# V of a pair of tiles as two-by-two blocks with seven products in place of eight

## The reference

```
q, k, v = heads(x @ Wq + bq), heads(x @ Wk + bk), heads(x @ Wv + bv)
scores  = einsum('bhqd,bhkd->bhqk', q, k) * scale
attn    = softmax(where(adj == 0, -inf, scores))
out     = einsum('bhqk,bhkd->bhqd', attn, v) as rows @ Wo + bo
result  = layernorm(x + out)          # eps 1e-5, no weight, no bias
```

## Time and profile before

| what | value |
|---|---|
| runs, median (lowest to highest) of 3 | 821.98 us (821.61 to 822.32) |
| the profiled execution | 821.39 us |
| its span, first to last instruction | 819.5 us |
| TensorE busy | 812.0 us, 99% |
| VectorE busy | 544.9 us, 66% |
| GpSimd busy | 512.6 us, 63% |
| ScalarE busy | 238.2 us, 29% |

### The profile page before, as it was taken

How to read it: one execution, slowest core, us unless ns; L and a number is a source line. 1 busy time by engine, 2 the same in 40 slices (tenths; PEclk the granted TensorE clock), 3 DMA queues, 4 the chain that set the end, 5 groups by cost and what they waited for, 6 DMA issues and landing times.

```text
span 819.5 us, 25422 instructions
## 1 busy us (share of the span) xinstructions
PE 812.0 (99%) x11286; PEld 665.1 (81%) x11286; DVE 544.9 (66%) x691; ACT 238.2 (29%) x315; POOL 512.6 (63%) x407
## 2 busy tenths in 40 slices
PE   9999999999999999999999999999999999999997
PEld 7788888888888888888888888888888888888886
DVE  5667667766567666676665776656766567766795
ACT  6532233221332222332223322133322233223223
POOL 1386667656675565856658566576665767657682
PEclk9999999999999999999999999999999999999999
DMA  9224424253342433424334243352424434234342
GB/s 321 90 79 122 120 81 135 84 143 95 88 143 72 149 92 92 139 70 142 105 91 134 71 144 95 82 154 82 128 88 106 136 82 131 84 108 118 105 105 104
DMA packets 50173, 92.37 MB, mean 113 GB/s; under 512 B 11280, under 2 KB 13328, under 8 KB 47888
## 3 DMA queue, kind: packets, MB, share of 16 engines
q1 hardware_dynamic: 47568, 87.08, 36.2%
q10 hardware_dynamic: 2496, 3.67, 1.6%
HBM read 40.37 MB, written 16.78 MB: 70 GB/s over the span
## 4 chain that ended last, share of the span: by engine, by line
PE 98%; DVE 1%; POOL 0%; ACT 0%; issue 0%; POOLq 0%; DVEq 0%
PE ring L289 23%; PE ring L291 21%; PE ring L290 21%; PE ring L386 7%; PE ring L387 7%; PE ring L390 7%; PE psum_s L357 6%; PE ring L375 6%; PE ring L407 1%; PE ring L309 0%; POOL soft L912 0%; PE ring L313 0%; PE ring L317 0%; DVE soft L717 0%; DVE top L724 0%; ACT soft L568 0%
## 5 line engine op out<-in xcount | busy, mean ns | idle before, releaser
L912 POOL TENSOR_TENSOR soft<-soft,top 128x1024 f32<-128x1024 f32 x62 | 125.2, 2020 | 77.5 <-DVE top L724 77.5
L171 POOL TENSOR_TENSOR soft<-soft,inverse 128x1024 f32<-128x1024 f32 x62 | 118.9, 1918 | 24.9 <-DVE inverse L731 22.2
L563 ACT ACTIVATE kt<-ring,bk 128x512 f32<-128x512 f32 x64 | 43.6, 681 | 258.7 <-PE ring L291 258.6
L889 POOL TENSOR_TENSOR x_lo<-x_raw,x_hi 128x512 fp32r<-128x512 f32 x56 | 72.0, 1286 | 61.1 <-ACT x_hi L548 61.1
L289 PE MATMUL ring<-wv_hi,x_hi 128*128 128x512 f32 x256 | 103.5, 404 | 0.0
L289 PE MATMUL ring<-x_hi,wk_hi 128*128 128x512 f32 x256 | 103.1, 403 | 0.0
L728 DVE TENSOR_REDUCE total<-soft 128x16 f32<-128x1024 f32 x62 | 75.6, 1219 | 41.0 <-ACT soft L568 41.0
L291 PE MATMUL ring<-wv_hi,x_lo 128*128 128x512 f32 x256 | 100.1, 391 | 0.0
L291 PE MATMUL ring<-x_hi,wk_lo 128*128 128x512 f32 x256 | 99.9, 390 | 0.0
L290 PE MATMUL ring<-x_lo,wk_hi 128*128 128x512 f32 x256 | 99.7, 390 | 0.0
L290 PE MATMUL ring<-wv_lo,x_hi 128*128 128x512 f32 x256 | 99.6, 389 | 0.0
(11 more groups left out here) (81 smaller groups left out, 1362.3 us busy)
## 6 DMA issues: line engine op xcount, KB each, us to landing
pt<-soft SPq DMA_DIRECT2D x464, 64.0 KB, 2.0
x_raw<-in_xt SPq DMA_DIRECT2D x15, 1024.0 KB, 6.8
row<-in_x SPq DMA_DIRECT2D x60, 256.0 KB, 2.7
out_rows<-row SPq DMA_DIRECT2D x60, 256.0 KB, 2.6
adj<-in_adj SPq DMA_DIRECT2D x16, 128.0 KB, 2.9
pt<-soft ACTq DMA_DIRECT2D x32, 64.0 KB, 2.2
kt<-in_wk SPq DMA_DIRECT2D x4, 256.0 KB, 5.1
row<-in_wv SPq DMA_DIRECT2D x1, 1024.0 KB, 8.4
```

The source lines that it names most:

```text
L171: ops.tensor_tensor(soft_of(c), soft_of(c), on_keys(inverse[:, c % 2, :]), ALU.mult).then_inc(normed, 1)
L889: nc.gpsimd.tensor_tensor(x_lo[:, buf, :, rows], x_raw[:, :, rows], x_hi[:, buf, :, rows].bitcast(F32), ALU.subtract).then_inc(x_lo_done, 1)
L912: nc.gpsimd.tensor_tensor(soft_of(c), soft_of(c), on_keys(top[:, c % 2, :]), ALU.subtract).then_inc(centred, 1)
```

## The change

For the pairs 1 to 27 (SEVEN), V of a pair is a product of two-by-two blocks: the rows of the two tiles by the two halves of the 512 input features, times the two halves of those by the two halves of the 512 output columns (HALF = 256). Seven block products, each of sums and differences of blocks, take the place of eight. One block product is six matmuls of 256 columns.

The sums of weights (t_raw, from Wv) are made once at the start by GpSimd (add_weights), in pt's space, cast by ScalarE and subtracted by VectorE. The sums of inputs are made for each pair: SP loads the pair's columns of the transposed x a second time (load_pair, 512 KB) into the two buffers of v that the pair will use (s_raw), VectorE makes four sums in place (add_inputs), ScalarE casts them into s_hi and GpSimd subtracts into s_lo (split_sums). The products go into psum_s, after the pair's masks have read it: first_products does five, last_products two, with project_out(a - 2) between them. VectorE adds them up in seven reads (read_first, read_middle, read_last). The next pair's scores wait for the last of them.

pt has two buffers in place of four (place(c) waits for mix(c - 2); the last six tiles use a part of kt besides), bias isn't repeated for the heads of a row group any more, and mask is done in two halves. The waits before project_k and project_q of the loop now count k_done and q_done, since V doesn't use those banks; the waits on v_done in the written-out end are counted anew (v_count).

```diff
+SEVEN = range(1, FULL)
...
+P1, P2, P4, P5, P6, P7, P3, PARTS = 1, 2, 3, 4, 5, 6, 7, 7
...
-        pt = sb("pt", [P, 4, 2, HEADS, SQ])
+        pt = sb("pt", [P, 2, 2, HEADS, SQ])
...
-        bias = sb("bias", [P, 2, GT, 2, KC, SQ])
+        bias = sb("bias", [P, 2, GT, 2, SQ])
...
+        def pt_of(c):
+            if c >= TILES - 6 and c // 2 % 2 == 1:
+                return kt[:, 0, c % 2 * 2:c % 2 * 2 + 2, :].rearrange("p q (h k) -> p q h k", k=SQ)
+            return pt[:, c % 2]
+        def pt_users(c):
+            return c - 3 if c >= TILES - 6 else c - 1
...
+        def s_raw(m):
+            return v[:, 2 * m % 4:2 * m % 4 + 2, :].rearrange("p t (c n) -> p (t c) n", n=2 * P)
...
+        def t_raw(n):
+            return pt[:, n // 2, n % 2, :, :].rearrange("p h k -> p (h k)").rearrange("p (c n) -> p c n", c=2)
...
-                wait_for(sp, mixed, c - 3)
+                wait_for(sp, mixed, pt_users(c))
...
+            def load_pair(m):
+                wait_for(sp, mixed, 2 * m - 2)
+                G, t = 2 * m // GT, 2 * m % GT
+                sp.dma_start(s_raw(m), xt_dram[G, :, :, t * P:(t + 2) * P]).then_inc(s_in[m % 2], DMA)
...
+            sp.wait_ge(t_raw_done, 4)
             load_row(0)
+            load_pair(1)
...
                 place(a)
                 load_row(b)
                 place(b)
+                if p >= 1 and p + 1 in SEVEN:
+                    load_pair(p + 1)
                 if p >= 1:
                     store(a - 2)
                 load_row(b + 1)
...
-                    wait_for(pe, masked, c)
+                    wait_for(pe, masked, 2 * c)
+                    if c // 2 > SEVEN.start:
+                        pe.wait_ge(v_read, v_reads(min(c // 2, SEVEN.stop)))
...
-                    pe.wait_ge(v_done, c + 2)
+                    if c // 2 in SEVEN:
+                        pe.wait_ge(v_read, v_reads(c // 2 + 1))
+                    else:
+                        pe.wait_ge(v_done, v_count(c + 1))
...
+            def product(out, left_hi, left_lo, right_hi, right_lo, adds=False):
...
+                for kc in range(2):
+                    nc.tensor.matmul(out, left_hi[:, kc, :], right_hi[:, kc, :], start=kc == 0 and not adds, stop=False,
+                                     skip_group_check=adds)
+                    nc.tensor.matmul(out, left_hi[:, kc, :], right_lo[:, kc, :], start=False, stop=False,
+                                     skip_group_check=adds)
+                    last = nc.tensor.matmul(out, left_lo[:, kc, :], right_hi[:, kc, :], start=False, stop=kc == 1,
+                                            skip_group_check=adds)
+                last.then_inc(v_part, 1)
...
+            def first_products(m):
+                pe.wait_ge(masked, 4 * (m + 1))
+                if m == SEVEN.start:
+                    pe.wait_ge(t_hi_done, 4)
+                    pe.wait_ge(t_lo_done, 4)
+                product(first_sums(), *inputs_block(m, 0, 0), *weights_block(0, 0))
+                product(second(0), *inputs_block(m, 0, 1), *weights_block(1, 0))
+                product(second(1), *inputs_block(m, 1, 1), *weights_sum(4))
+                pe.wait_ge(s_hi_done, m - SEVEN.start + 1)
+                pe.wait_ge(s_lo_done, m - SEVEN.start + 1)
+                product(other_sums(), *inputs_sum(1), *weights_sum(1))
+                pe.wait_ge(v_read, v_reads(m) + P1)
+                product(first_sums(), *inputs_sum(2), *weights_sum(2), adds=True)
+            def last_products(m):
+                pe.wait_ge(v_read, v_reads(m) + P6)
+                product(first_sums(), *inputs_sum(3), *weights_sum(3), adds=True)
+                product(other_sums(), *inputs_sum(4), *weights_block(1, 1), adds=True)
...
                 wait_for(pe, row_added, a - 2)
                 mix(a - 2)
                 mix(b - 2)
-                pe.wait_ge(k_done, b + 5)
-                project_v(a)
-                pe.wait_ge(q_done, b + 5)
-                project_v(b)
+                first_products(p)
                 pe.wait_ge(ot_lo_done, p)
                 project_out(a - 2)
+                last_products(p)
                 project_out(b - 2)
...
+            def split_sums(m):
+                act.wait_ge(s_raw_done, 4 * (m - SEVEN.start + 1))
+                wait_for(act, v_part, v_reads(m))
+                nc.scalar.copy(s_hi[:, :, :], s_raw(m)).then_inc(s_hi_done, 1)
...
+                if p + 1 in SEVEN:
+                    split_sums(p + 1)
...
+            def add_inputs(m):
+                x, done = s_raw(m), 4 * (m - SEVEN.start)
+                dve.wait_ge(s_in[m % 2], DMA * ((m - SEVEN.start) // 2 + 1))
+                nc.vector.tensor_tensor(at(x, 1, 1), at(x, 1, 0), at(x, 1, 1), ALU.add).then_inc(s_raw_done, 1)
+                dve.wait_ge(s_raw_done, done + 1)
+                nc.vector.tensor_tensor(at(x, 1, 0), at(x, 0, 0), at(x, 1, 0), ALU.subtract).then_inc(s_raw_done, 1)
+                dve.wait_ge(s_raw_done, done + 2)
+                nc.vector.tensor_tensor(at(x, 0, 0), at(x, 1, 1), at(x, 0, 0), ALU.subtract).then_inc(s_raw_done, 1)
+                dve.wait_ge(s_raw_done, done + 3)
+                nc.vector.tensor_tensor(at(x, 0, 1), at(x, 0, 1), at(x, 0, 0), ALU.subtract).then_inc(s_raw_done, 1)
...
+            def read_first(m):
+                dve.wait_ge(v_part, v_reads(m) + P1)
+                dve.wait_ge(s_lo_done, m - SEVEN.start + 1)
+                nc.vector.tensor_tensor(quarter(m, 0, 0), first_sums(), bias_of(0), ALU.add).then_inc(v_read, 1)
+            def read_middle(m):
+                dve.wait_ge(v_part, v_reads(m) + P2)
+                dve.wait_ge(v_read, v_reads(m) + P1)
+                nc.vector.tensor_tensor(quarter(m, 0, 0), second(0), quarter(m, 0, 0), ALU.add).then_inc(v_read, 1)
+                dve.wait_ge(v_part, v_reads(m) + P4)
+                nc.vector.tensor_tensor(quarter(m, 1, 0), second(1), bias_of(0), ALU.add).then_inc(v_read, 1)
+                dve.wait_ge(v_part, v_reads(m) + P5)
+                nc.vector.tensor_tensor(quarter(m, 1, 1), other_sums(), bias_of(1), ALU.add).then_inc(v_read, 1)
+                dve.wait_ge(v_part, v_reads(m) + P6)
+                nc.vector.tensor_tensor(quarter(m, 0, 1), first_sums(), bias_of(1), ALU.add).then_inc(v_read, 1)
+            def read_last(m):
+                both = v[:, (2 * m + 1) % 4, :].rearrange("p (t n) -> p t n", t=2)
+                dve.wait_ge(v_part, v_reads(m) + P7)
+                dve.wait_ge(v_read, v_reads(m) + P6)
+                nc.vector.tensor_tensor(both, first_sums().unsqueeze(1).to_broadcast([P, 2, HALF]), both,
+                                        ALU.add).then_inc(v_read, 1)
+                dve.wait_ge(v_part, v_reads(m) + P3)
+                nc.vector.tensor_tensor(quarter(m, 0, 1), other_sums(), quarter(m, 0, 1), ALU.add).then_inc(v_read, 1)
...
-                nc.vector.tensor_tensor(
-                    soft_of(c).rearrange("p b (r c) k -> p b r (c k)", r=HC),
-                    psum_s[:, :, c % 2].rearrange("p r b c k -> p b r (c k)"),
-                    bias[:, c // GT % 2, c % GT].rearrange("p b c k -> p b (c k)").unsqueeze(2)
-                    .to_broadcast([P, 2, HC, KC * SQ]),
-                    ALU.add).then_inc(masked, 1)
-                dve.wait_ge(masked, c + 1)
+                for b in range(2):
+                    nc.vector.tensor_tensor(
+                        soft_of(c)[:, b].rearrange("p (r c) k -> p r c k", r=HC), psum_s[:, :, c % 2, b],
+                        bias[:, c // GT % 2, c % GT, b].unsqueeze(1).unsqueeze(1).to_broadcast([P, HC, KC, SQ]),
+                        ALU.add).then_inc(masked, 1)
+                dve.wait_ge(masked, 2 * c + 2)
                 nc.vector.tensor_reduce(top[:, c % 2, :], by_row_head(soft_of(c)), AX_XY, ALU.max).then_inc(topped, 1)
...
                 if p >= 2:
                     norm_row(dve, nc.vector, a - 3)
+                if p == 0:
+                    split_weight_sums()
                 sum_up(a)
                 sum_up(b)
                 turn(a)
+                if p >= 1:
+                    read_first(p)
+                    split_ot(p - 1)
                 turn(b)
                 if p >= 1:
-                    split_ot(p - 1)
-                read_v(a)
-                read_v(b)
+                    read_middle(p)
+                else:
+                    read_v(a)
+                    read_v(b)
                 if p >= 1:
-                    add_row(a - 2)
+                    add_y(a - 2)
+                    read_last(p)
+                    row_sums(a - 2)
                     norm_row(dve, nc.vector, a - 2)
+                if p + 1 in SEVEN:
+                    add_inputs(p + 1)
             T = TILES
...
             def make_bias(G):
                 pool.wait_ge(adj_in, DMA * (G + 1))
                 if G >= 2:
-                    pool.wait_ge(masked, GT * (G - 1))
```

(86 more changed lines are left out.)

46 lines of the change are left out of this document (29 added, 17 removed).

## The result

| | before | after |
|---|---|---|
| median of 4 runs each (lowest to highest), us | 822.15 (821.61 to 823.01) | 987.38 (983.8 to 991.9) |
| the profiled execution, us | 821.39 | 987.18 |
| its span, us | 819.5 | 985.1 |
| ratio of the times, 95% interval | | 1.2011 [1.1961, 1.2062] |

What follows compares the result with a forecast made beforehand. TensorE, 99% busy, bounds the kernel at 25.18 us a pair. Profiled execution 821.4 + 3.2 start + 128.8 (25 x 5.15) - 1.5 end = 951.9; with 0.6 for the median 952.5, said as 953 us, range 880 to 1025.

Steps and rivals of the forecast that it cites:

- The gain on TensorE: In V of each pair: seven products take 5.15 us, 0.44 less per pair, 11.9 us for 27 pairs.
- The step that decides: On SP's in-order queue: load_pair behind place(b) closes a chain of waits of 30.33 us per pair, 5.15 more than 25.18.
- sixteen issues and a row: SP issuing place(a), load_row and place(b) before the next load_pair: 11.45 us, plus 0.05 to the next issue.
- The landing: Transfer time of load_pair's 512 KB: 4.1 us, interpolated between 256 KB and 1 MB, range 2.7 to 6.8.
- It doesn't bind, by 1.4 us: place(a)'s wait for mix(a-2), with two pt buffers: mix ends at 11.5 us, turn(a) at 12.9, so no delay.
- The queue ahead of load_pair, then, is the delay, and nothing else: On SP: the issues ahead of load_pair are the only delay in the chain of waits; place(a) adds no second wait.
- three signs of being wrong: Prediction wrong if load has landed by add_inputs, sixteen issues take 6 us, or granted clock drops below 1.00 in loop.
- The clock rival: TensorE's idle gaps lower its clock; project_q takes 5.0 us, 31 to 36 us a pair, 1043 us; 9 in 100.
- Start and end: mask(4) starts 3.2 us later (0 to 6); pair 27, without add_inputs behind it, is short by about 1.5 us.
- The load is hidden anyway: Load always landed in time; VectorE and TensorE alternate at 25.05 us a pair: 820.5 us, about no change; 7 in 100.
- ring through TensorE: Chain of waits from add_inputs through mask(a), project_q, mix, products and project_out back to VectorE's norm_row: 25.05 us a pair.
- TensorE sets the pace: SP's issues go through in half the time, chain of waits under 24.74 us a pair: faster, 811 us; 7 in 100.

Runs made afterwards that it cites:

- filled run: The changed kernel with twelve unused matmuls put into TensorE's gap before project_q(b+4), the wait for row_added moved ahead of them: 956.2 us, ratio 1.1648.
- clock low and four buffers: The kernel before with load_pair added behind place(b) and add_inputs at the end of VectorE's round, the sums unused: 953.0 us, ratio 1.1578.
- best order: The changed kernel with load_pair and load_row(b) ahead of place(a), add_inputs between row_sums and norm_row, weights' subtractions ahead of mask(0): 818.85 us, ratio 0.9952.

## Why the prediction was right, and where it was off

**The gain on TensorE** was right: 5.15 us for V of a pair, 0.120 us between starts. The row of before was the measure to take. The 262 cycles of the Trainium skill (TensorE: Matmul & The Clock Gate, Back-to-back issue gap), by estimate 109 ns at 2.4 GHz, are not the pace of any stage here. What the forecast left out is a third of that gain. Two changes from products of 256 columns to ones of 512 go with 0.05 us more in project_out: its first step is 0.24 us in the rows above (416.75 to 416.99), where a step was 0.227 before. The scores lose 0.09, all of it between their own matmuls (1.47 us from the first start to the last, before 1.38), not at a change of stage; what causes that isn't shown.

**The step that decides** was right in place and mechanism. Moving one call returns 131 us, and adding that call and add_inputs to the old kernel costs 130 (128.8 forecast for the rounds). Its terms held: add_inputs 1.80 as said, mask to turn 10.96 for 11.22, sixteen issues and a row 11.61 for 11.50. The landing was interpolated too short, 4.84 for 4.1. That the sum of the filled run, 30.29, comes so near 30.33 is partly luck: its landing is 0.47 us longer than forecast, and add_row, the stretch from mask to turn and the issues are 0.10 to 0.26 shorter.

**The step that failed** is "It doesn't bind, by 1.4 us", and with it "The queue ahead of load_pair, then, is the delay, and nothing else". The sum behind it took project_q(b+4) at 2.72 us. It had, in its own rival on the clock, the number that speaks against it: 5.0 at the lower level. Measured are 3.90 in the mean and up to 5.42, a place(a) late in 14 of 25 rounds, 0.57 us behind turn(a) in the mean of all, and a round of 31.4. Of the prediction's own three signs of being wrong this is the one that appeared: the granted clock dropped below 1.00 in the loop. The clock rival was right that the clock falls and that mix then passes turn(a); it was wrong that all products stay slow until the next add_inputs: from 413.00 to 423.00 the clock is 1.00. So a round of 31.4 us is at the lower edge of its 31 to 36, far from the 34 that its 1043 us took. Three runs bear that out together: clock held and two buffers 956 us, clock low and four buffers (without the products) 953, both 987; and two buffers in the old kernel are free. How the 1.09 us between the change and the filled run divide is in the table, 0.47 for place(a), 0.27 for the landing and 0.35 for the issues. Why the last two differ stays open: within the change they are nearly the same in the 14 rounds with a late place(a), 5.0 and 11.7 us, as in the other 11, 4.8 and 11.5.

**Start and end.** The 3.2 us for the start were 7.1: 4.2 already at mask(2) (53.57, before 49.34), where the four subtractions of the weights' sums took 4.21 us, not 2.76, and 2.9 more behind the first two add_inputs. In the best order, with the subtractions ahead of mask(0), it is 2.4. The end, forecast 1.5 us shorter, came out between 0.8 shorter (filled run) and 1.8 longer; no run was made for that.

**The rivals.** "The load is hidden anyway" described the kernel with both loads early, 820.5 us forecast and 822.3 measured. But it left out load_row(b): an early load_pair alone gives 857, not 820. Whether its ring through TensorE, 25.05 us, is what holds that run isn't told apart, since the rounds there (24.96) are only 0.07 above those of the best order. "TensorE sets the pace" came true in the best order, at 818.85 and not at 811, by a gain of 7.1 us in the 25 rounds where 11.9 was taken for 27 pairs, and by the start and the end, 3.9 us later and longer where 1 was allowed.

## What to carry to other kernels

A transfer put into an in-order queue is worth what stands ahead of it: count the issue time of all that is in front, and follow what it feeds back to that same queue. If the way closes, its length is the new round, and after one such ring is opened the next is looked for (here load_row, 34 us) before a number is given. And when a forecast makes the bounding engine idle, its stages after the gap are priced at the lower clock, above all where a buffer has been given up in the same change.

## What the runs showed of the hardware

Some of VectorE's operations between tiles in SBUF take longer beside a GpSimd operation that began before them, and end 0.3 to 0.6 us behind it: norm_row, begun 0.07 us behind s_lo, took 2.60 us for 0.55, and one of the weights' subtractions in the changed kernel, where GpSimd's centre ran, 2.4 for 0.68 (ns, least, median and most of the four):

```profile
L902 DVE TENSOR_TENSOR t_lo<-pt,t_hi x4: 679/681/2405, 38.0 to 41.5; 128x512 fp32r<-128x512 f32 x4
```

A mask, which reads PSUM, took 1.29 us beside s_lo as it does elsewhere, and the maximum, which reads one tile in SBUF, 1.22, also as elsewhere. The Trainium skill (GPSIMD Engine Reference, Specifications) says that GpSimd shares its SBUF interfaces with VectorE. The rows of norm_row and the subtraction agree; no run here shows which operand decides. s_lo itself takes 2.39 us where centre, with as many elements, takes 1.92; what sets that wasn't tried.
